# A fused attention and mixture-of-experts kernel: gathered tiles turned in 32x32 blocks on VectorE instead of on TensorE

## The reference, cut to what matters

```python
xn = _layernorm(x, axis=-1)
x = x + attention(xn, ...) + moe(xn, Wg, w1, w2)

# moe, with S = 4096 tokens, E = 8 experts, K = 2, C = 1280 slots an expert
probs = softmax(xr @ Wg);  gate_vals, expert_idx = top_k(probs, K)
# dispatch_mask[e, c]: which (token, choice) fills slot c of expert e
dispatched = xr[dispatch_mask.reshape(-1) % S].reshape(E, C, d)
h = relu(einsum('ecd,edf->ecf', dispatched, w1))     # w1: 8 x 512 x 2048
expert_out = einsum('ecf,efd->ecd', h, w2)           # w2: 8 x 2048 x 512
# every token gets its two experts' rows back, weighted by the gates
```

## Time and profile before

| | us |
|---|---|
| runs of the kernel before | 2173.14, 2175.56, 2176.17 (median 2175.56) |
| profiled execution, its own time | 2182.53 |
| its span, first to last instruction | 2180.8 |
| mean granted TensorE clock | 0.988 of full speed |

### The profile page before, as it was taken

The page is one execution under the profiler, slowest core; times in us unless marked ns, Lnnn a source line. Parts: engine busy times, 40 slices in busy tenths (PEclk is TensorE's granted clock), DMA queues, the critical chain, the costliest instruction groups (busy, mean ns, idle before and its releaser), DMA issues.

```text
span 2180.8 us, 28220 instructions
## 1 busy us (share of the span) xinstructions
PE 2110.3 (97%) x11672; PEld 1741.4 (80%) x11672; DVE 765.1 (35%) x1486; ACT 573.5 (26%) x1017; POOL 477.6 (22%) x372
## 2 busy tenths in 40 slices
PE   6899999999979999999999999999999999999997
PEld 4787788778768888878887887888888888878886
DVE  5555565555454113312422322331232124223311
ACT  5222322332233212312312321231232123113211
POOL 2524442443350111020211202101010202111011
PEclk9899999999989999999999999999999999999998
DMA  4220212011025122321622413332141215224021
GB/s 151 77 78 31 70 60 78 21 60 60 32 68 198 26 49 67 118 44 44 159 28 62 111 60 68 74 111 30 52 113 59 40 49 144 42 55 112 28 30 20
DMA packets 83964, 151.39 MB, mean 69 GB/s; under 512 B 16768, under 2 KB 16768, under 8 KB 83824
## 3 DMA queue, kind: packets, MB, share of 16 engines
q1 hardware_dynamic: 63424, 105.65, 14.6%
q0 software_dynamic: 20400, 43.74, 11.4%
HBM read 109.82 MB, written 39.53 MB: 68 GB/s over the span
## 4 chain that ended last, share of the span: by engine, by line
PE 86%; DMA 5%; DVE 3%; issue 2%; POOL 2%; ACT 1%; SPq 0%; POOLq 0%; ACTq 0%; DVEq 0%
PE bank L1074 43%; PE bank L1349 29%; PE bank L1211 4%; DMA out_rows<-y,add_row 4%; PE bank L1081 3%; PE bank L1387 2%; POOL out_rows L564 1%; PE bank L1158 1%; DMA gathered<-xn_rows,gather_row 1%; PE bank L1175 1%; PE bank L1200 1%; DVE xnT_lo L801 1%; PE bank L1122 1%; PE bank L1194 1%; PE bank L1168 0%
## 5 line engine op out<-in xcount | busy, mean ns | idle before, releaser
L1026 DVE SCALAR_TENSOR_TENSOR h_lo<-bank,h_hi 128x512 fp32r<-128x512 f32 x256 | 177.1, 692 | 788.2 <-ACT h_hi L741 788.2
L1074 PE MATMUL bank<-xT_hi,w_hi 128*128 128x512 f32 x1024 | 406.6, 397 | 0.5 <-issue 0.5
L1074 PE MATMUL bank<-xT_hi,w_lo 128*128 128x512 f32 x1024 | 399.6, 390 | 0.0
L1349 PE MATMUL bank<-w_hi,h_lo 128*128 128x512 f32 x1024 | 398.6, 389 | 0.0
L1074 PE MATMUL bank<-xT_lo,w_hi 128*128 128x512 f32 x1024 | 398.5, 389 | 0.0
L1349 PE MATMUL bank<-w_hi,h_hi 128*128 128x512 f32 x1024 | 398.3, 389 | 0.0
L1349 PE MATMUL bank<-w_lo,h_hi 128*128 128x512 f32 x1024 | 398.3, 389 | 0.0
L741 ACT ACTIVATE h_hi<-bank 128x512 fp32r<-128x512 f32 x256 | 153.1, 598 | 823.5 <-PE bank L1074 823.5
L564 POOL DMA_INDIRECT out_rows<-y,add_row x80 | 128.8, 1611 | 777.0 <-ACT y L734 704.9
L1074 PEld LDWEIGHTS bank<-xT_hi,w_lo 128*128 128x128 f32 x1024 | 192.2, 188 | 41.6
L1349 PEld LDWEIGHTS bank<-w_lo,h_hi 128*128 128x128 f32 x1024 | 192.2, 188 | 39.9
(11 more groups left out here) (185 smaller groups left out, 2434.8 us busy)
## 6 DMA issues: line engine op xcount, KB each, us to landing
raw_weights<-in_L_ffn_w SPq DMA_DIRECT2D x256, 256.0 KB, 4.1
x_in<-in_L_attn_x SPq DMA_DIRECT2D x32, 256.0 KB, 3.2
xn_rows<-xn SPq DMA_DIRECT2D x32, 256.0 KB, 2.2
x_res<-in_L_attn_x SPq DMA_DIRECT2D x32, 256.0 KB, 4.6
out_rows<-y_attn SPq DMA_DIRECT2D x32, 256.0 KB, 2.0
gathered<-xn_rows,gather_row POOLq DMA_INDIRECT x80, 3.5
out_rows<-y,add_row POOLq DMA_INDIRECT x80, 5.1
attn_raw<-in_L_attn_Wq SPq DMA_DIRECT2D x4, 256.0 KB, 7.8
```

Of the source, the lines that this page charges most:

```text
L1026: v_.scalar_tensor_tensor(h_lo[f % 2][:, 0:n * P], h_bank[f % 2][:, 0:n * P], 0.0, h_hi[f % 2][:, 0:n * P].bitcast(F32), ALU.max, ALU.subt ...
L1074: last = mm(dest, at(left[l], t), at_r(right[r], t), start=(i == 0), stop=(i == n - 1))
L1349: last = mm(y_bank[i][:, :], hx[f % 2][:, part], wx[c][:, f % FPC, :], start=(f == 0 and l == 0), stop=(f == FT - 1 and l == 2))
```

## The change

A gathered tile is fetched in four indirect DMAs instead of one. Each fetches 128 pieces of 512 B, a quarter of a row, from `xn_rows` seen as 16384 pieces; which piece goes to which partition is chosen so that transposing all 32x32 blocks of the tile on VectorE (one instruction, into the new tile `x_blocks`) leaves each partition with one column number of the tokens. The columns then lie in another order over partitions and k tiles than before, so the rows of each `w1` unit are loaded in the matching order (four strips of 32 rows); `w2`'s source is written in the same form, with its rows in the old order. `gather_rows` makes four row numbers a slot, with one operation on the whole tile and 16 on strips of 32 partitions. TensorE no longer turns gathered tiles; ScalarE and VectorE read `x_blocks` in SBUF in place of the PSUM bank. The turns' places move to f = 5, 7, ..., 15 and f = 6, 9, 12, 15. GpSimd starts the next expert's first two gathers before it confirms the last spare block. In the attention tail the turns move from TensorE's program to VectorE's.

```diff
+QUADS = P // 32
+    xn_pieces = xn_dram.rearrange("t (q c) -> (t q) c", q=QUADS)
-        gather_row = sb("gather_row", [P, SLOT_TILES], I32)
+        gather_base = sb("gather_base", [P, SLOT_TILES])
+        gather_row = sb("gather_row", [P, SLOT_TILES, QUADS], I32)
+        x_blocks = esb("x_blocks", [P, D])
...
-                return dict(zip(range(3, FT, 2), tiles))
+                return dict(zip(range(5, FT, 2), tiles))
             if j == LAST and follows:
-                return dict(zip(range(4, FT, 3), [(i, 0) for i in range(BLOCKS[0])]))
+                return dict(zip(range(6, FT, 3), [(i, 0) for i in range(BLOCKS[0])]))
...
             if i < FPC:
-                return w1[e, i * P:(i + 1) * P, c * D:(c + 1) * D]
+                return w1[e].rearrange("(q t d) f -> t q d f", q=QUADS, t=DT)[i, :, :, c * D:(c + 1) * D]
             first = (c * FPC + i % FPC) * P
-            return w2[e, first:first + P, :]
+            return w2[e, first:first + P, :].rearrange("(q d) n -> q d n", q=QUADS)
...
+        def token_cols(xT, i):
+            return xT[:, :, i * P:(i + 1) * P].rearrange("p t (q c) -> p t q c", q=QUADS)
+        def by_k_tile(blocks):
+            return blocks[:, :].rearrange("p (q t c) -> p t q c", q=QUADS, t=DT)
...
-                    pool.indirect_dma_start(xg[:, nth % 2, :], None, xn_dram[:, :],
-                                            bass.IndirectOffsetOnAxis(ap=gather_row[:, col:col + 1], axis=0),
-                                            bounds_check=TOKENS - 1, oob_is_err=False).then_inc(x_gathered[nth % 2], 16)
+                    for i in range(QUADS):
+                        pool.indirect_dma_start(xg[:, nth % 2, i * P:(i + 1) * P], None, xn_pieces,
+                                                bass.IndirectOffsetOnAxis(ap=gather_row[:, col, i:i + 1], axis=0),
+                                                bounds_check=QUADS * TOKENS - 1, oob_is_err=False).then_inc(x_gathered[nth % 2], 16)
...
                 for j in range(LAST):
                     scatter(e, j)
-                    confirm(e, j)
+                    if j < LAST - 1:
+                        confirm(e, j)
                 if e < EXPERTS - 1:
                     pool.wait_ge(S["gather_rows_ready"], e + 2)
-                    gather(e + 1, 0)
+                    gather(e + 1, 0, (0, 1))
+                confirm(e, LAST - 1)
+                if e < EXPERTS - 1:
+                    gather(e + 1, 0, (2, 3))
...
             def turned_high(m, j, i):
                 act.wait_ge(S["x_turned"], m + 1)
-                a.copy(xT_hi[j][:, :, i * P:(i + 1) * P],
-                       xt_bank[(FIRST[j] + i) % 2][:, :].rearrange("p (t c) -> p t c", t=DT)).then_inc(S["xT_hi_made"], 1)
+                a.copy(token_cols(xT_hi[j], i), by_k_tile(x_blocks)).then_inc(S["xT_hi_made"], 1)
...
-                v_.tensor_scalar(gather_row[:, :], slot_rec[:, :, 0], float(TOKENS - 1), None, ALU.min).then_inc(S["gather_rows_ready"], 1)
+                step(v_.tensor_scalar(gather_base[:, :], slot_rec[:, :, 0], float(TOKENS - 1), float(QUADS), ALU.min, ALU.mult))
+                for q in range(QUADS):
+                    for i in range(QUADS):
+                        last = v_.tensor_scalar(gather_row[q * 32:(q + 1) * 32, :, i], gather_base[i * 32:(i + 1) * 32, :],
+                                                float(q), None, ALU.add)
+                last.then_inc(S["gather_rows_ready"], 1)
+
+            def turn_gathered(m, j, i):
+                slot = (FIRST[j] + i) % 2
+                uses = m // SLOT_TILES * (SLOT_TILES // 2) + (FIRST[j] + i) // 2 + 1
+                dve.wait_ge(x_gathered[slot], 16 * QUADS * uses)
+                wait(dve, ("xT_lo_made", m))
+                v_.transpose(x_blocks[:, :], xg[:, slot, :]).then_inc(S["x_turned"], 1)
+                dve.wait_ge(S["x_turned"], m + 1)
...
-            turned_low(0, 0, 0)
-            turned_low(1, 0, 1)
+            for i in range(2):
+                turn_gathered(i, 0, i)
+                turned_low(i, 0, i)
             scale_heads(ATTN_UNITS - 1)
             oT_low(ATTN_UNITS - 1)
-            turned_low(2, 0, 2)
-            turned_low(3, 0, 3)
+            for i in range(2, BLOCKS[0]):
+                turn_gathered(i, 0, i)
+                turned_low(i, 0, i)
...
                         if f in turn:
                             i, nj = turn[f]
+                            turn_gathered(SLOT_TILES * e + SLOT_TILES * (nj == 0) + FIRST[nj] + i, nj, i)
                             turned_low(SLOT_TILES * e + SLOT_TILES * (nj == 0) + FIRST[nj] + i, nj, i)
...
-            turn_gathered(0, 1, 0, 0)
-            turn_gathered(1, 1, 0, 1)
...
-            turn_gathered(2, 2, 0, 2)
-            turn_gathered(3, 2, 0, 3)
...
-                        if f in turn_here:
-                            i, nj = turn_here[f]
-                            nth = FIRST[nj] + i
-                            turn_gathered(SLOT_TILES * e + SLOT_TILES * (nj == 0) + nth,
-                                          SLOT_TILES // 2 * e + SLOT_TILES // 2 * (nj == 0) + nth // 2 + 1, nj, i)
```

More of the change, by code:

```diff
@@ L925, in gather_rows @@
                 dve.wait_ge(S["rec_loaded"], 32 * (e + 1))
-                v_.tensor_scalar(gather_row[:, :], slot_rec[:, :, 0], float(TOKENS - 1), None, ALU.min).then_inc(S["gather_rows_ready"], 1)
+                step(v_.tensor_scalar(gather_base[:, :], slot_rec[:, :, 0], float(TOKENS - 1), float(QUADS), ALU.min, ALU.mult))
[11 more added lines that the diff above has]
+                dve.wait_ge(S["x_turned"], m + 1)
             def turned_low(m, j, i):
                 dve.wait_ge(S["xT_hi_made"], m + 1)
-                part = slice(i * P, (i + 1) * P)
-                v_.tensor_tensor(xT_lo[j][:, :, part], xt_bank[(FIRST[j] + i) % 2][:, :].rearrange("p (t c) -> p t c", t=DT),
-                                 xT_hi[j][:, :, part].bitcast(F32), ALU.subtract).then_inc(S["xT_lo_made"], 1)
+                v_.tensor_tensor(token_cols(xT_lo[j], i), by_k_tile(x_blocks), token_cols(xT_hi[j], i).bitcast(F32),
+                                 ALU.subtract).then_inc(S["xT_lo_made"], 1)
             norm_pair(0)
@@ L1041, in main @@
                         if j == LAST and f == 0 and follows:
-                            wait(dve, *[(s, 16 * (SLOT_TILES // 2) * (e + 1)) for s in x_gathered])
+                            wait(dve, *[(s, 16 * QUADS * (SLOT_TILES // 2) * (e + 1)) for s in x_gathered])
                             gather_rows(e + 1)
@@ L1214, in project_out @@
                     last.then_inc(S["out_projected"], 1)
[L1216 to L1221, removed]
             pe.wait_ge(S["consts_made"], 6)
@@ L1330, in main @@
                     xT = (xT_hi[j], xT_lo[j])
-                    turn_here = turns(j, follows)
                     def up(f):
```

## The result

The changed kernel took 2162.18 us (median of 4 runs, 2161.84 to 2162.40) where the kernel before took 2174.35 us beside it: ratio 0.9943, 95% interval 0.9926 to 0.996, so 12.2 us or 0.6% faster, where 30.6 us were forecast. The kernel after agrees between the two measurements to 1.6 us; the kernel before does not (5 us). All its later medians, on three chips, are 2178.9 to 2181.1 us, so the 2174.35 stands alone, and why is open.

What follows compares the result with a forecast made beforehand. TensorE was taken to bound the expert stage, a VectorE, GpSimd and ScalarE chain the stretch from 600 to 656 us. Terms -37 - 10.5 + 12.6 + 1.8 + 2.5 = -30.6 us gave 2145 us, range 2130 to 2180.

Steps and rivals of the forecast that it cites:

- The weight loads: w1's rows come from four strips, each row still 2 KB; by the nearest row, a 256 KB load, no cost.
- rival 1: Weight loads use fewer DMA engines: w1 alone 2153 us, expert 0 losing about 8; w2 too, 2252 us; chance 0.20.
- -23 us if it holds for w1 alone: Forecast sum if the skill's rule, engines dividing the outermost dimension, narrows only w1's loads; +76 us if w2's too.
- Turns: TensorE's turns of gathered tiles removed: 76 that count, at 0.49 us each, 37 us gained.
- Moved places: Later turns and gathers ahead of the last confirm end TensorE's gather waits in the expert stage: 10.5 of 10.9 us gained.
- margin of nearly 7 us: After the last empty spare-block scatter, the fourth gather lands at 976 us; its turn is due at 982.8.
- VectorE in the expert stage: Block transpose (0.69 us taken) and list operations fit in 3.9 us of slack before the down product: no cost.
- Rival 2: VectorE becomes late through late gathers or a slow transpose, delaying h_lo: 2162 us, up to 2171; chance 0.10.
- The head: Before expert 0, longer list and more gathers move its start from 655.55 to 668.15 us: 12.6 us lost (11.9 to 13.3).
- Residual sums: At expert 0's start, VectorE's last four residual sums follow the turns, delaying stores, weight loads and splits: 1.8 us lost.
- Lower clock: After standing still some 8 us before expert 0, TensorE runs at 1.2 GHz: 2.5 us lost, bounds 0 and 6.
- Rival 3: No change, 2175 us: expert 0's head would have to cost 47 us, as if no gathers overlapped; chance 0.05.

Runs made afterwards that it cites:

- moved_four_gathers: before_moved with each tile fetched by four gathers of 512 B pieces, old layout, still turned on TensorE: 2189.26 us, ratio 1.0037 to the kernel before.
- before_moved: The kernel before with only the turns' new places and the next expert's gathers ahead of the last confirm: 2169.45 us against 2181.08, ratio 0.9949.
- four_strips: The kernel after with each w1 tile loaded by four transfers of 32 rows instead of one: 2153.91 us, ratio 0.9874 to the kernel before.
- strips_old_places: The kernel after with the turns' old places, old order of confirm and gathers, and w1 by four transfers: 2152.96 us, ratio 0.9884 to the kernel before.
- before_w1_source: The kernel before with one line changed, w1's tile loaded from a source seen as 4 x 32 x 512: 2217.88 us, ratio 1.0175.

## Why the prediction was wrong

The direction was right, the size was not: -30.6 us forecast, -12.2 and -16 measured. Two terms make the difference, one chosen wrongly and one that wasn't there.

**The step that failed: "The weight loads ... By the nearest row, nothing."** The nearest row was a load of the same bytes and the same 2 KB rows, but with 128 rows in one run; what the change altered was just what that row did not have, a source of four strips. The right answer stood in the same text as the milder form of rival 1: w1 alone narrow, steady experts unharmed, expert 0 about 8 us later. The sign that the forecast named for it is there: from 640 us on ScalarE waits 80.5 us for raw weights, in the kernel before 5.5. The runs put its cost at 10 us by time: 8.1 us of it in the expert stage (1476.92 to 1468.79), where the wait fell from 7.1 to 0.9 us and the lower clock's share from 4.4 to 1.9 us. w2's loads stayed wide, as that form said (0.99 from 692 to 695 us), and experts 1 to 7 don't stall. That its 8 us came so close is in part luck: it reckoned 3.1 us a load and a loss summed up over 24 loads; here w1's first loads land 4.1 to 4.3 us apart, and the whole loss is one wait behind the first three.

The rule of the Trainium skill ("DMA: Bandwidth & Descriptors", "Why a DMA increments its semaphore by 16 and not by 1") that was cited against this step has the trace with it for w1: a source whose outermost dimension is 4 keeps the DMA engines 0.27 busy. For w2 the trace shows no such thing: its view in the program has a 4 outermost too, but its rows lie one behind another, and its loads keep the engines 0.99 busy. The forecast's "-23 us if it holds for w1 alone" is 7 us from the second measurement; the next term is 4.9 of them.

**The term that was missing: the end.** No row behind the last matmul was read. GpSimd's closing DRAIN went from 3.09 to 8.03 us, +4.94 us, and moved_four_gathers has the same with only the gathers cut in four. With both terms the forecast's sum is -30.6 + 8.1 + 4.9 = -17.6 us (-15.7 with the loads' 10 us by time). The second measurement gave -16 us, the first -12.2; the rest of the first is the 5 us by which the kernel before was faster there.

The other steps, in its order:

- **Turns, -37.** Right. From before_moved to four_strips the expert stage falls by 34.25 us; 1.7 us more of lower clock and 0.9 us of wait stand against that: 36.9 us, over 76 turns 0.485 each (0.49 forecast).
- **Moved places, -10.5.** Right for the kernel before: -11.6 us by time, -12.0 by the expert stage of second profiles. In the changed kernel this gain would have come without the move, had the loads been wide (strips_old_places); beside narrow ones the move is worth 9 us. The "margin of nearly 7 us" was enough: no wait for a gather in experts 1 to 7.
- **VectorE in the expert stage, nothing.** Right: transpose 0.70 us (0.69 taken), and twice that costs nothing. Rival 2 has fallen; that it named 2162 us, the time first measured, is chance.
- **The head, +12.6 (11.9 to 13.3).** Right in itself: list to start of expert 0 took 32.07 us, forecast were 32.25 (635.90 to 668.15). As a difference it is 12.4 by the first profiles and 14.1 by the second, since the head of the kernel before was 19.65 us in its first profile and 18.12 in its second. List 3.1 us (3.4 taken), pitch 1.30 to 1.31 (1.3), from the start of the last transpose to that of expert 0 2.21 us (2.25 taken from the landing). It started at 664.60, not near 668, since this execution's list started 3.4 us sooner.
- **Residual sums, +1.8.** In four_strips a wait of 0.9 us is left at this place, half of the 1.8; but there the three splits before it still come 1.8 us apart, so how much of it is the sums' is not shown.
- **Lower clock, +2.5.** About right: some ten matmuls 0.43 us apart behind expert 0's start, 2.1 us in the kernel after and 1.9 in four_strips.

Rival 3 has fallen with the head's measured price, far under 47 us.

## What to carry to other kernels

When a rearranged source gives a transfer a small outermost dimension, look at the DMA share of a stretch in which only such transfers run: here 0.27 instead of about 1. Four transfers in place of one gave 0.56, as far as their issue allowed, and 10 us with it. Look at the share and not at the form alone: w2's view had the same small dimension and stayed wide. A price taken from "the nearest row" tells little if that row lacks the very property that the edit changes; here the other bound was the better guess. Work that pays in the steady state can be left out where it stands in a chain: expert 0 done the old way and the rest the new way beat the kernel after by 25 and the kernel before by 41 us; and read the profile's last rows too, behind the last product.

## What the runs showed of the hardware, unexpected

- GpSimd's closing DRAIN took 3.09 us with 80 gathers (four profiles), 2.11 with 160, 5.99 with 280 and ten single ones, 8.03 with 320 (seven profiles), each time to the nanosecond. It changes with the gathers issued (moved_four_gathers has little else beside before_moved), but not in proportion; by which rule, stays open.
- Narrow weight loads slow what shares the DMA engines: with the whole set at the same share of 0.61, gathers landed 7.9 instead of 3.7 us after their issue in one stretch, 4.3 instead of 3.5 over all 80 (medians).
- A wait of TensorE can cost more than itself: behind nine of the 13 waits in before_w1_source stands a stretch at half clock, mostly 1.5 to 1.7 us lost in each and 2.9 behind the one of 7.7 us; in the kernel after 2.2 us behind the one of 7.1 us. But it need not: two waits of 2.6 and 3.0 us there, and all four of 1.6 to 2.6 us in the first profile of the kernel before, have none behind them.
